# Two pairs of score banks in turn, a mask written by TensorE, an expert split in the attention steps, and another order in the last layer

## The chip, the cores and the metric

One NeuronCore of a Trainium2 chip runs the whole program. The metric is the device time of one execution in microseconds (us). TensorE (PE) multiplies, VectorE (DVE), ScalarE (ACT) and GpSimd (POOL) do the elementwise work, SyncE (SP) only issues DMAs. Each engine runs its own instruction list in order and waits for the others on semaphores. PSUM, into which TensorE writes, has eight banks of 128 x 512 float32.

## The reference

The input is x (1024 tokens of 256 values, four sequences of 256), token ids and a context of four 256 x 256 matrices. Four blocks are added to x in turn, each on a layer-normalised input:

```
x = x + experts_by_token_id(norm(x), ctx)          # stage A: silu(x.W)*(x.W) @ W, 4 experts
x = x + [attention(16 heads of 16, causal) + MoE(8 experts of 512, best 2)](norm(x))   # B, M
x = x + wkv_recurrence(norm(x), ctx)               # stage C: scans over 256 positions
x = x + bitlinear(gelu(bitlinear(norm(x), w1)), w2)  # stage D: 256 -> 1024 -> 256
```

In the attention, scores above the diagonal are minus infinity before the softmax. In stage D each row of the input and of the gelu's output is scaled by 127 over its largest magnitude and rounded.

## The kernel before

Tokens are cut into 8 tiles of 128. Every engine has its program written out by hand. There is no planner, so an instruction runs when all before it in its engine's list have and its semaphores stand.

**Attention (about 90 to 245 us).** The four sequences are batches b, with 8 pairs of heads each. That makes 32 pairs r. For each pair the scores are computed twice. `score_row_pair(r)` (L1477) writes q.k with queries on the partitions, and `row_max` (L1037) on DVE adds the causal mask and takes each row's maximum, four instructions per pair. All row pairs of batch 0 use banks 0 and 1, those of the other batches banks 2 and 3 (`row_banks`, L380), and a row pair waits until the maxima of the one before it are done. When a batch's 16 heads are done, `max_rows(b)` (L1466) transposes the maxima, `nm_copy` (L759) on ACT negates them, and SP's `store_max` (L449) writes them by DMA as one more row of the packed q. `score_col_pair(r)` (L1495) then gives the transposed scores less their maximum, ACT exponentiates them into `E_sb` (L773), POOL sets the part above the diagonal to 0 (L593 and L595, 2 instructions per head), and `weighted_values` (L1510) multiplies by v.

**The steps.** The first `LEAD` = 12 row pairs run ahead. Then come steps m = 0 to 39 (L1584 on PE, the same loop on the other engines): transposed scores of pair m, row pair m + 12, and for each batch that is finished an epilogue. The epilogue turns the output (`ep_turn_o`, first step of the next batch), divides, turns (`ep_turn_h`, second), multiplies by Wo (`ep_out`, third), normalises (POOL's rs at L603, DVE's x_n at L1139), turns again (`ep_turn_x`, fifth) and computes the router's logits (`ep_logits`, sixth). `max_rows` of batches 1 to 3 stands in steps 4, 12 and 20. DVE splits the weights of experts 0 and 1 into a high and a low part in quarters (`split_piece`, L1154, steps 16 to 19 and 24 to 27). POOL splits expert 2 after the last step (L606).

**Router, MoE and recurrence (245 to 472 us).** DVE and PE sort the tokens by expert, POOL gathers 23 blocks of 128 rows by indirect DMA, PE multiplies each by its expert's weights in three products (L1366 to L1368).

**Stage D (472 to 513 us).** Per tile: DVE normalises and scales (`d_scales`, L1304), POOL rounds (`d_round`, L642), PE turns (`d_h_turn`), ACT copies (`d_h_copy`), PE multiplies by w1 (`d_up_products`), ACT applies gelu, DVE scales, POOL rounds, PE turns (`d_g_turn`), ACT copies (`d_g_copy`), PE multiplies by w2 (`d_down_products`), DVE adds (`d_last`). PE's order in a step is turn, up, down of three tiles back, g turn of two tiles back (L1774). DVE does the scales of tile s and of the gelu output s - 2 in one call.

Of the kernel before, what the change touches and what calls it, by code (L numbers as in the profile page):

```python
# [15 lines left out]
def mixed_block_kernel(nc, x, ids, ctx_t, wqkv_t, wo_t, wr_t, wexp, ln1, ln2, decay, decay_row, bonus, w1_t, w2_t, out):  # L16
    F = mybir.dt.float32
    R = mybir.dt.float32r
    BF = mybir.dt.bfloat16
# [6 lines left out]
    P = 128  # L26
# [25 lines left out]
    with ctx:  # L52
# [23 lines left out]
        causal = sb(base, "causal", [P, 2 * P])  # L76
        iota_p = sb(base, "iota_p", [P, P])
# [100 lines left out]
        junk = sb(scope_b, "junk", [P, 2, 3 * P], BF)  # L178
# [38 lines left out]
        Q_FIRST = 1e-15  # L217
        w_exp = sb(scope_c, "w_exp", [P, KC])
# [6 lines left out]
        q_h = sb(scope_c, "q_h", [P, 2, D])  # L225
# [3 lines left out]
        q_top = sb(scope_c, "q_top", [P, NT + 2, 2])  # L229
        q_unit = sb(scope_c, "q_unit", [P, NT + 2, 2])  # L230
        q_inv = sb(scope_c, "q_inv", [P, NT + 2, 2])
        q_deq = sb(scope_c, "q_deq", [P, NT + 2, 2])
# [67 lines left out]
        mask_done = sem("mask_done")  # L300
# [49 lines left out]
        d_inv = sem("d_inv")  # L350
        d_deq = sem("d_deq")
# [19 lines left out]
        NM_AT = {(b + 1) * HP - LEAD: b for b in range(1, B)}  # L371
# [3 lines left out]
        SPLIT_AT = [2 * HP, 3 * HP]  # L375
        EP_OT, EP_HT, EP_WO, EP_RMS, EP_XT, EP_LG = 1, 2, 3, 4, 5, 6
# [3 lines left out]
        def row_banks(b):  # L380

            return bank[0:2] if b == 0 else bank[2:4]
# [16 lines left out]
        G_LAG = 2  # L399
# [9 lines left out]
        def _(sp):  # L409
# [85 lines left out]
        def _(pool):  # L495
# [24 lines left out]
            g.memset(causal[:, :], 0.0)  # L520
            g.memset(picked[:, :, :], 0.0)
# [22 lines left out]

            link(g.affine_select(out=causal[:, P:2 * P], in_=causal[:, P:2 * P], compare_op=ALU.is_ge,
# [41 lines left out]
            for m in range(NP + HP):  # L587
                if m < NP:
                    for n in (2 * m, 2 * m + 1):
                        pool.wait_ge(exp_done, n + 1)  # L590
                        diag = E_sb[:, n % E_RING, :]
# [13 lines left out]
            pool.wait_ge(st_done, B * H)  # L605
            split_expert(RING - 1)  # L606
# [35 lines left out]
            def d_round(step):  # L642
                if step < NT:
                    pool.wait_ge(d_inv, step + 1)
                    g.tensor_scalar(q_h[:, step % 2, :], q_h[:, step % 2, :], q_inv[:, step, 0:1], MAGIC,
                                    ALU.mult, ALU.add).then_inc(d_hr, 1)
                i = step - G_LAG
                if i >= 0:
                    pool.wait_ge(d_inv, step + 1)
                    g.tensor_scalar(q_g[:, i % 3, :], q_g[:, i % 3, :], q_inv[:, step, 1:2], MAGIC,  # L650
                                    ALU.mult, ALU.add).then_inc(d_gr, 1)
# [15 lines left out]
            for i in range(2, 4):  # L667
                rsqrt(4, i).then_inc(rstd_in[4], 1)
            for step in range(NT + G_LAG):
                d_round(step)  # L670
                if step < 2:
                    rsqrt(4, step + 4).then_inc(rstd_in[4], 1)
                if step == 1:
# [1159 lines left out]
```

## Time and profile before

| what | us |
|---|---|
| median of three runs (lowest to highest) | 510.27 (509.72 to 516.72) |
| the profiled execution, its span | 516.34, 514.6 |
| busy: PE, DVE, POOL, ACT | 369.4, 261.3, 222.3, 152.8 |
| the chain that ended last: PE, DVE, POOL, issue | 53%, 18%, 10%, 7% |
| mean granted TensorE clock | 0.793 of full |

The span is from the first instruction to the last. "Busy" adds up what ran on an engine. The chain follows the last instruction back through whatever released each step, so its shares say on which engine the time lies, while a busy engine beside the chain costs nothing. The granted clock is 1.0 where TensorE ran at 2.4 GHz and 0.5 at 1.2 GHz. In square brackets a timeline row gives the idle time before an instruction and what ended it.

### The profile page before, as it was taken

How to read it: one execution, taken by the hardware profiler on the slowest of the kernel's cores; microseconds unless marked ns; L12 is line 12 of the kernel's file. 1: busy time of each engine (PE TensorE's matmuls, PEld its weight loads, DVE VectorE, ACT ScalarE, POOL GpSimd, SP SyncE). 2: the span in 40 equal slices, each digit the busy share in tenths (PEclk: the TensorE clock that was granted, in tenths of full speed). 3: DMA queues.
4: the chain of work that ended last, by engine and by line, in shares of the span. 5: the costliest groups of instructions: out<-in, count | busy, mean ns of one | idle time of the engine just before them, and what ended most of it. 6: DMA issues, size and time to landing. Idle time of an engine off the chain costs nothing.

```text
span 514.6 us, 6681 instructions
## 1 busy us (share of the span) xinstructions
PE 369.4 (72%) x2042; PEld 282.0 (55%) x2045; DVE 261.3 (51%) x780; ACT 152.8 (30%) x332; POOL 222.3 (43%) x338
## 2 busy tenths in 40 slices
PE   0776999648797877764353399999999535757765
PEld 0555787326565655443342288887788314646454
DVE  4578896654354672514720032333232157998652
ACT  2221243113342425410020134333243311233563
POOL 2482443402232444615277208676930188423530
PEclk9997899757757667755556599999999955786799
DMA  8900029967180004000033334326000132000011
GB/s 260 394 11 1 0 94 155 150 138 120 44 120 25 3 2 144 20 1 20 1 84 109 52 121 176 134 79 221 34 26 29 37 90 62 1 1 0 4 37 42
DMA packets 16693, 39.18 MB, mean 76 GB/s; under 512 B 3314, under 2 KB 10804, under 8 KB 14868
## 3 DMA queue, kind: packets, MB, share of 16 engines
q1 hardware_dynamic: 11476, 30.63, 22.3%
q0 software_dynamic: 1872, 5.11, 3.9%
q10 hardware_dynamic: 3312, 3.02, 1.7%
q8 instruction: 18, 0.29, 0.2%
q14 instruction: 15, 0.12, 0.1%
HBM read 29.38 MB, written 9.31 MB: 75 GB/s over the span
## 4 chain that ended last, share of the span: by engine, by line
PE 53%; DVE 18%; POOL 10%; issue 7%; DMA 5%; ACT 4%; another core or an unknown queue 2%; SPq 1%; ACTq 0%; DVEq 0%; POOLq 0%
PE bank L1366 8%; PE bank L1368 7%; PE bank L1367 7%; PE bank L1372 6%; DVE junk L1045 4%; PE bank L1428 3%; POOL yc L629 3%; PE bank L1489 3%; PE bank L1553 3%; PE bank L1462 2%; PE bank L1525 2%; PE bank L1739 2%; PE bank L1537 2%; PE bank L1758 1%
## 5 line engine op out<-in xcount | busy, mean ns | idle before, releaser
L1241 DVE TENSOR_TENSOR act_lo<-bank,act_hi 128x512 fp32r<-128x512 f32 x23 | 15.9, 692 | 84.9 <-ACT act_hi L815 74.4
L1045 DVE CUSTOM_DVE_ANT_0 junk<-bank,causal 128x128 bf16<-128x128 f32 (+1 forms) x128 | 38.0, 354 | 28.0 <-PE bank L1489 28.0
L593 POOL TENSOR_SCALAR_AFFINE_SELECT E_sb<-E_sb 128x128 f32<-128x128 f32 x64 | 21.3, 333 | 71.5 <-ACT E_sb L773 71.4
L1366 PE MATMUL bank<-we_hi,xg_hi 128*128 x92 | 39.7, 432 | 9.8 <-DVE xg_lo L1235 8.2
L584 POOL TENSOR_TENSOR we_lo<-we_lo,we_hi 128x3072 fp32r<-128x3072 f32 x6 | 40.8, 6798 | 0.5
L1367 PE MATMUL bank<-we_lo,xg_hi 128*128 x92 | 37.3, 405 | 0.0
L1368 PE MATMUL bank<-we_hi,xg_lo 128*128 x92 | 37.2, 404 | 0.0
L1366 PE MATMUL bank<-we_hi,act_hi 128*128 x92 | 28.9, 314 | 10.7 <-DVE act_lo L1241 10.7
L773 ACT ACTIVATE E_sb<-bank 128x384 f32<-128x384 f32 x64 | 27.9, 488 | 24.0 <-PE bank L1507 22.6
L583 POOL TENSOR_SCALAR we_hi<-we_lo 128x3072 fp32r<-128x3072 f32 x6 | 17.0, 2828 | 36.3 <-DMA we_lo<-in_wexp 36.2
L629 POOL DMA_INDIRECT yc<-y_dram,pos_i x16 | 15.9, 991 | 35.7 <-DMA y_dram<-y_sb 31.7
L1489 PE MATMUL bank<-k_pack,q_pack 48*128 48x256 f32 (+1 forms) x128 | 20.8, 413 | 14.0 <-DVE negmax L1045 13.9
L613 POOL DMA_INDIRECT xg<-xn_dram,slot_tok x23 | 22.0, 958 | 17.2 <-DVE slot_tok L1219 10.5
L1368 PE MATMUL bank<-we_hi,act_lo 128*128 x92 | 26.5, 288 | 0.0
L1367 PE MATMUL bank<-we_lo,act_hi 128*128 x92 | 26.5, 288 | 0.0
L1489 PEld LDWEIGHTS bank<-k_pack,q_pack 48*128 48x128 f32 x128 | 13.0, 251 | 24.2 <-DVE negmax L1045 18.1
L1366 PEld LDWEIGHTS bank<-we_hi,act_hi 128*128 128x128 f32 x92 | 17.9, 195 | 15.1 <-issue 14.9
L1366 PEld LDWEIGHTS bank<-we_hi,xg_hi 128*128 128x128 f32 x92 | 18.1, 196 | 12.8 <-issue 10.4
L1248 DVE TENSOR_TENSOR act_m<-sil,bank 128x512 f32<-128x512 f32 x23 | 15.8, 688 | 15.3 <-remote 10.0
L811 ACT ACTIVATE sil<-bank 128x512 f32<-128x512 f32 x23 | 13.8, 598 | 32.7 <-PE bank L1368 25.8
L806 ACT ACTIVATE xg_hi<-bank 128x256 fp32r<-128x256 f32 x23 | 8.8, 384 | 46.3 <-PE bank L1372 34.4
L595 POOL TENSOR_SCALAR_AFFINE_SELECT E_sb<-E_sb 128x128 f32<-128x128 f32 x64 | 21.3, 333 | 0.0
(246 smaller groups left out, 1002.7 us busy)
## 6 DMA issues: line engine op xcount, KB each, us to landing
we_lo<-in_wexp SPq DMA_DIRECT2D x8, 1536.0 KB, 7.1
qk_dram<-qk_parts SPq DMA_DIRECT2D x8, 512.0 KB, 4.3
q_pack<-qk_dram SPq DMA_DIRECT2D x24, 128.0 KB, 4.6
k_pack<-qk_dram SPq DMA_DIRECT2D x24, 128.0 KB, 7.8
y_dram<-y_sb ACTq DMA_DIRECT2D x23, 128.0 KB, 1.7
we_hi<-in_w_t SPq DMA_DIRECT2D x2, 1024.0 KB, 11.1
ctx_sb<-in_ctx_t SPq DMA_DIRECT2D x1, 1024.0 KB, 5.4
xn_dram<-x_n SPq DMA_DIRECT2D x8, 128.0 KB, 1.8
```

The source lines that it names most:

```text
L584: g.tensor_tensor(lo, lo.bitcast(F), hi.bitcast(F), ALU.subtract).then_inc(split_done, 1)
L593: g.affine_select(out=diag[:, 0:P], in_=diag[:, 0:P], compare_op=ALU.is_ge, fill=0.0, base=0, pattern=[[1, P]], channel_multiplier=-1)
L595: g.affine_select(out=diag[:, 2 * P:3 * P], in_=diag[:, 2 * P:3 * P], compare_op=ALU.is_ge, fill=0.0, base=0, pattern=[[1, P]], channel_mu ...
L613: g.indirect_dma_start(xg[:, s, :], None, xn_dram, bass.IndirectOffsetOnAxis(slot_tok[:, s:s + 1], 0))\
L629: g.indirect_dma_start(yc[:, i % YB, c, :], None, y_dram, bass.IndirectOffsetOnAxis(pos_i[:, c, i:i + 1], 0))\
L773: a.activation(E_sb[:, n % E_RING, :], bank[4 + n % 2][:, 0:3 * P], ACT.Exp).then_inc(exp_done, 1)
L1045: last = v.tensor_tensor_reduce(out=junk[:, m % 2, t * P:t * P + keys], in0=row_banks(b)[h % 2][:, t * P:t * P + keys], in1=causal[:, 2 * ...
L1366: t_.matmul(dst, l_hi, r_hi, start=start, stop=False)
L1367: t_.matmul(dst, l_hi, r_lo, start=False, stop=False)
L1368: return t_.matmul(dst, l_lo, r_hi, start=False, stop=stop)
L1372: last = t_.transpose(dst[:, k * P:(k + 1) * P], src[:, k * P:(k + 1) * P], ident[:, :] if idt is None else idt)
L1489: last = t_.matmul(row_banks(b)[odd][:, t * P:t * P + (t + 1) * P], q[parts[odd], j, t * P:(t + 1) * P], k[parts[odd], j, 0:(t + 1) * P], ...
```

## The change

1. **Row pairs.** The 12 row pairs ahead use banks 0/1 and 2/3 in turn, and a row pair waits only for the maxima of the pair two before it. From row pair 12 on banks 2/3 are used, each after the one before. `max_rows` writes into bank 7 and stands one step later (5, 13, 21), with waits for what else uses that bank. In the part ahead, `b_low(5)`, `b_norm(6)`, `b_norm(7)` on DVE and `b_turn(6)`, `b_turn(7)` on PE move behind more row pairs.
2. **Mask.** `score_col_pair` first writes the mask into each of the two banks with a bf16 product of the identity and a constant 128 x 384 matrix (0 or -1e30), and the scores are accumulated on it. POOL's 128 instructions on `E_sb` go. POOL makes the constant at the start (one memset, two selects).
3. **Epilogue.** `ep_turn_x` and `ep_logits` stand one step later (sixth and seventh).
4. **Expert 2.** Its load is issued once the transposed scores of batch 1 are done, and DVE splits experts 0, 1, 2 in steps 18 to 21, 22 to 25, 26 to 29. POOL's split of it goes.
5. **Stage D.** The input's scales are separate from those of the gelu output and run three tiles ahead on three buffers. PE's order in a step is g turn, turn of the next tile, down, up of the next tile, and ACT's is gelu, copy of the next tile, g copy.

The added wait on `nm_row` in the diff stands in `ep_logits`; the last two blocks are DVE's and PE's loops of stage D.

```diff
+        causal_t = sb(base, "causal_t", [P, 3 * P], BF)
-        NM_AT = {(b + 1) * HP - LEAD: b for b in range(1, B)}
+        NM_AT = {(b + 1) * HP - LEAD + 1: b for b in range(1, B)}
-        SPLIT_AT = [2 * HP, 3 * HP]
-        EP_OT, EP_HT, EP_WO, EP_RMS, EP_XT, EP_LG = 1, 2, 3, 4, 5, 6
+        SPLIT_AT = [2 * HP + 2, 2 * HP + 6, 3 * HP + 2]
+        EP_OT, EP_HT, EP_WO, EP_RMS, EP_XT, EP_LG = 1, 2, 3, 4, 6, 7
+        def row_banks(r):
+            return bank[0:2] if r < LEAD and r % 2 == 0 else bank[2:4]
+        def row_bank_free(r):
+            return 2 * (r - 1) if r < LEAD else 2 * r
...
             store_max(2)
             for i in range(TB):
                 store_x2(i)
+            sp.wait_ge(st_done, 2 * H)
+            load_expert(RING - 1)
             store_max(3)
...
-            sp.wait_ge(st_done, 3 * H)
-            load_expert(RING - 1)
...
+            g.memset(causal_t[:, :], 0.0)
+            for c in (0, 2):
+                g.affine_select(out=causal_t[:, c * P:(c + 1) * P], in_=causal_t[:, c * P:(c + 1) * P],
+                                compare_op=ALU.is_ge, fill=-BIG, base=0, pattern=[[1, P]], channel_multiplier=-1)
...
-                if m < NP:
-                    for n in (2 * m, 2 * m + 1):
-                        pool.wait_ge(exp_done, n + 1)
...
-                        g.affine_select(out=diag[:, 0:P], in_=diag[:, 0:P], compare_op=ALU.is_ge, fill=0.0,
-                                        base=0, pattern=[[1, P]], channel_multiplier=-1)
-                        g.affine_select(out=diag[:, 2 * P:3 * P], in_=diag[:, 2 * P:3 * P], compare_op=ALU.is_ge,
-                                        fill=0.0, base=0, pattern=[[1, P]], channel_multiplier=-1)\
-                            .then_inc(mask_done, 1)
...
-            pool.wait_ge(st_done, B * H)
-            split_expert(RING - 1)
...
-                if r >= 1:
-                    pe.wait_ge(max_done, 2 * r)
+                if r == 1:
+                    pe.wait_ge(a_y_in, NT)
+                elif r >= 2:
+                    pe.wait_ge(max_done, row_bank_free(r))
...
                 for odd in range(2):
-                    t_.matmul(bank[4 + odd][:, 0:S], k[parts[odd], j, 0:P], q[parts[odd], j, :], start=True, stop=True)
+                    t_.matmul(bank[4 + odd][:, 0:3 * P], ident_b[:, :], causal_t[:, :], start=True, stop=False)
+                for odd in range(2):
+                    t_.matmul(bank[4 + odd][:, 0:S], k[parts[odd], j, 0:P], q[parts[odd], j, :], start=False, stop=False)
...
-                pe.wait_ge(mask_done, 4 * g + 4)
+                pe.wait_ge(exp_done, 4 * g + 4)
...
+                pe.wait_ge(nm_row, min(bt + 3, B))
...
-            for r in range(5, HP):
+            for r in range(2, 9):
                 score_row_pair(r)
             max_rows(0)
-            for r in range(HP, LEAD):
-                score_row_pair(r)
+            score_row_pair(9)
+            b_turn(6)
+            score_row_pair(10)
+            b_turn(7)
+            score_row_pair(11)
...
+            for i in range(NT + 2):
+                if i < NT:
+                    d_g_scales(i)
+                if i + H_AHEAD < NT:
+                    d_h_scales(i + H_AHEAD)
+                if i >= 2:
+                    d_last(i - 2)
...
-                if step < NT:
-                    d_h_turn(step)
-                    d_up_products(step)
-                if step >= G_LAG + 1:
-                    d_down_products(step - G_LAG - 1)
-                if G_LAG <= step < NT + G_LAG:
-                    d_g_turn(step - G_LAG)
+                if 2 <= step < NT + 2:
+                    d_g_turn(step - 2)
+                if step + 1 < NT:
+                    d_h_turn(step + 1)
+                if step >= 3:
+                    d_down_products(step - 3)
+                if step + 1 < NT:
+                    d_up_products(step + 1)
```

## Rows read from the trace of the kernel before

**Rows 1.** Stages: start:end, span, busy PE, PEld, DVE, ACT, POOL; clock; DMA share; GB/s
```profile
90.00:116.50 26.50, 13.77 (x66) 8.58 (x66) 16.18 (x96) 3.51 (x6) 5.90 (x8) 0.63 0.78 144
116.50:222.00 105.50, 86.95 (x600) 59.53 (x598) 52.08 (x246) 40.25 (x93) 40.54 (x130) 0.69 0.27 57
258.00:292.00 34.00, 11.88 (x46) 9.51 (x46) 4.88 (x16) 4.50 (x8) 22.03 (x23) 0.60 0.38 89
292.00:407.00 115.00, 110.93 (x645) 92.98 (x646) 36.36 (x63) 39.58 (x85) 53.54 (x18) 0.99 0.27 95
472.00:514.00 42.00, 27.91 (x171) 19.00 (x174) 21.88 (x56) 21.59 (x41) 13.12 (x16) 0.87 0.07 26
```

**Rows 2.** Timeline 20 to 60 us, POOL and DVE: start, length, instruction, idle before
```profile
27.79 0.28 POOL L545 TENSOR_SCALAR_AFFINE_SELECT causal<-causal 128x128 f32<-128x128 f32 x1
...
35.39 0.43 DVE L923 BATCH_NORM_STATS2 stat<-x_sb 128x6 f32<-128x256 f32 x1 [1.29 <-POOL x_sb L562]
```

**Rows 3.** Page, costliest groups: busy, mean ns, idle before and its releaser
```profile
L1045 DVE CUSTOM_DVE_ANT_0 junk<-bank,causal 128x128 bf16<-128x128 f32 (+1 forms) x128 | 38.0, 354 | 28.0 <-PE bank L1489 28.0
```

**Rows 4.** Timeline 100 to 120 us, TensorE and the sync queue
```profile
107.04 0.79 PE L1489 MATMUL bank<-k_pack,q_pack 48*128 48x128 f32 x4 [1.29 <-DVE negmax L1045]
...
109.13 0.60 PE L1469 MATMUL bank<-ident,negmax 128*16 128x128 f32 x2 [1.29 <-DVE negmax L1045]
...
116.50 0.42 PE L1505 MATMUL bank<-q_pack,k_pack 49*128 49x256 f32 x2
...
110.16 1.46 SPq L453 DMA_DIRECT2D q_pack<-negmax_t  x2
```

**Rows 5.** Waits 117 to 245 us: who waited for whom, us, times, longest
```profile
PE bank L1372 <- DVE x_n L1139: 10.1, 2, 6.7
...
PE bank L1469 <- DVE negmax L1045: 7.3, 3, 2.7
...
PE bank L1525 <- POOL E_sb L595: 2.2, 2, 1.7
```

**Rows 6.** Timeline 180 to 192 us, the step before the maxima are turned
```profile
188.28 0.35 DVE L1131 SCALAR_TENSOR_TENSOR rs_tmp<-mv 128x1 f32<-128x1 f32 x2
...
189.79 0.60 PE L1469 MATMUL bank<-ident,negmax 128*16 128x128 f32 x2 [2.74 <-DVE negmax L1045]
```

**Rows 7.** Timeline 478 to 486 us, TensorE: bf16 products at either clock
```profile
478.70 1.89 PE L1739 MATMUL bank<-w1q,q_ht 128*128 128x512 bf16 x4 [0.47 <-ACT q_ht L883]
...
483.75 1.04 PE L1739 MATMUL bank<-w1q,q_ht 128*128 128x512 bf16 x4 [1.03 <-ACT q_ht L883]
484.62 1.04 PE L1758 MATMUL bank<-w2q,q_gt 128*128 128x256 bf16 x8
```

**Rows 8.** Timeline 212 to 250 us, DVE and POOL: normalised rows, gate, split
```profile
215.31 0.92 DVE L1139 SCALAR_TENSOR_TENSOR x_n<-res,rs,ln_row 128x256 f32<-128x256 f32 x2 [0.58 <-POOL rs L603]
...
237.75 3.37 DVE L1139 SCALAR_TENSOR_TENSOR x_n<-res,rs,ln_row 128x256 f32<-128x256 f32 x2 [1.09 <-POOL rs L603]
...
245.77 1.89 DVE L1179 TENSOR_TENSOR gate<-top 128x8 f32<-128x8 f32 x1
...
248.83 0.17 DVE L1191 TENSOR_TENSOR gate<-gate 128x8 f32<-128x8 f32 x1
...
237.80 3.05 POOL L583 TENSOR_SCALAR we_hi<-we_lo 128x3072 fp32r<-128x3072 f32 x1
```

**Rows 9.** Timeline 485 to 510 us, the last layer: DVE, ACT, TensorE
```profile
485.77 1.22 DVE L1316 TENSOR_REDUCE q_top<-q_g 128x1 f32<-128x1024 f32 x1 [1.96 <-ACT q_g L892]
...
487.76 0.41 DVE L928 TENSOR_SCALAR q_h<-x_sb,mv,rs 128x256 f32<-128x256 f32 x1
...
486.57 1.09 ACT L900 ACTIVATE q_gt<-bank 128x512 bf16<-128x512 f32 x2 [0.83 <-PE bank L1372]
...
487.99 1.04 PE L1739 MATMUL bank<-w1q,q_ht 128*128 128x512 bf16 x3 [1.24 <-ACT q_ht L883]
...
507.75 1.05 PE L1758 MATMUL bank<-w2q,q_gt 128*128 128x256 bf16 x8 [1.18 <-ACT q_gt L900]
```

More of the change, by code:

```diff
@@ L217, in mixed_block_kernel @@
         Q_FIRST = 1e-15
+        H_AHEAD = 3
+        H_BUF = 3
         w_exp = sb(scope_c, "w_exp", [P, KC])
@@ L666, in _ @@
             c_times_v(3)
-            for i in range(2, 4):
+            for i in range(2, 5):
                 rsqrt(4, i).then_inc(rstd_in[4], 1)
[L669 to L673, printed above, removed]
-                    for i in range(6, 8):
-                        rsqrt(4, i).then_inc(rstd_in[4], 1)
+            for i in range(H_AHEAD):
+                d_round_h(i)
+                rsqrt(4, i + 5).then_inc(rstd_in[4], 1)
+            for i in range(NT):
+                d_round_g(i)
+                if i + H_AHEAD < NT:
+                    d_round_h(i + H_AHEAD)
         @block.scalar
@@ L762, in nm_copy @@
                     act.wait_ge(nm_in[b - 1], 32)
-                a.activation(negmax_t[:, :], row_banks(b)[0][0:H, 0:S], ACT.Copy, scale=-1.0).then_inc(nm_row, 1)
+                a.activation(negmax_t[:, :], bank[EP_Z][0:H, 0:S], ACT.Copy, scale=-1.0).then_inc(nm_row, 1)
             nm_copy(0)
+            b_turned(6)
+            b_turned(7)
             for m in range(NP + HP):
@@ L902, in d_g_copy @@
                 last.then_inc(d_gtc, 1)
-            for step in range(NT + G_LAG):
+            d_h_copy(0)
+            for step in range(NT + 2):
                 if step < NT:
-                    d_h_copy(step)
                     d_gelu_of(step)
-                if step >= G_LAG:
-                    d_g_copy(step - G_LAG)
+                if step + 1 < NT:
+                    d_h_copy(step + 1)
+                if step >= 2:
+                    d_g_copy(step - 2)
         @block.vector
@@ L1097, in _ @@
             b_low(4)
-            b_norm(6)
-            b_stats(7)
-            row_pair(1)
-            row_pair(2)
-            b_low(5)
-            row_pair(3)
+            row_pair(1)
+            b_stats(7)
+            for r in range(2, 6):
+                row_pair(r)
+            b_low(5)
+            for r in range(6, 8):
+                row_pair(r)
+            b_norm(6)
+            row_pair(8)
             b_norm(7)
-            for r in range(4, LEAD):
+            for r in range(9, LEAD):
                 row_pair(r)
@@ L1349, in _ @@
                 c_result(i)
[L1350 to L1357 removed]
+                if i < 4 + H_AHEAD:
+                    d_h_scales(i - 4)
+            for i in range(NT + 2):
+                if i < NT:
+                    d_g_scales(i)
+                if i + H_AHEAD < NT:
+                    d_h_scales(i + H_AHEAD)
+                if i >= 2:
+                    d_last(i - 2)
         @block.tensor
@@ L1467, in max_rows @@
                 pe.wait_ge(max_done, H * (b + 1))
+                if b == 0:
+                    pe.wait_ge(b_lo, 6)
+                elif b == 1:
+                    pe.wait_ge(b_lo, 2 * B)
+                else:
+                    pe.wait_ge(ep_htc, b - 1)
                 for t in range(TB):
-                    last = t_.transpose(row_banks(b)[0][0:H, t * P:(t + 1) * P], negmax[:, b % 2, t, :], ident[:, :])
+                    last = t_.transpose(bank[EP_Z][0:H, t * P:(t + 1) * P], negmax[:, b % 2, t, :], ident[:, :])
                 last.then_inc(nm_tr, 1)
```

109 lines of the change are left out of this document (44 added, 65 removed).

## The prediction

> **What bounds the kernel now.** I read the stages first, then the waits, then the timelines of the stretches that the change touches. By stage [rows 1], TensorE is busy for 110.93 of 115 us in the experts at nearly full clock. Nothing in the change touches that, and the 34 us at their start belong to gathers and waits that it leaves alone. Three stretches are loose. In the row pairs ahead of the steps (90 to 116.5 us) PE is busy for 13.8 of 26.5 us. In the steps (116.5 to 222) it is busy for 87 of 105.5 us at a mean clock of 0.69, so PE mostly sets the pace, and its work there is dear. In the last layer it is busy for 28 of 42 us. The reader should see why each is loose. Ahead of the steps PE and DVE take turns: a row pair starts every 2.09 us (107.04 to 109.13), 1.29 of them spent waiting for maxima [rows 4]. In the steps PE's waits are few and have names [rows 5]. After the last step DVE works beside a long POOL split and is slow [rows 8].
>
> **Base.** The sum is made against the profiled execution, 516.34 us with a span of 514.6. It is 6.1 us above the median of 510.27, which two of the three runs are near. I take the difference between the kernels off the median.
>
> **1. Two bank pairs: -6.2 us.** DVE needs 38.0 us for 32 pairs of maxima, 1.19 us a pair [rows 3]. With two bank pairs PE's 0.8 us [rows 4] fit beside that. The first two pairs don't gain, since PE runs a projection product between pair 1 and pair 2 as before, and counting back five periods from 107.04 puts pair 2 at 97 and its maxima at 97.6. From there DVE has six pairs and one 0.7 us copy until batch 0's maxima are done: 97.6 + 7.1 + 0.7 = 105.5, against 109.1 before. Then come the transposes 0.6, the copy 0.4, the issue 1.46 (before at 110.16), and a landing, which no row shows for so small a transfer. The nearest is 1.7 us for 128 KB. That gives 109.7. The DMA engines are 78% busy here [rows 1] with the packed heads, so I take 110.3 for the first transposed scores, which before started at 116.50. Bounds: 4 (the row waits behind all the head loads) to 7.5 (it does not wait). The norms and turns of tiles 6 and 7 lie under DVE's and PE's slack. Their users (steps 1 and 3) come more than 6 us later, and if they were late the product at step 1 would be what waits.
>
> **2. Maxima turned a step later: -4.0 us.** PE waited 7.3 us for the maxima at steps 4, 12 and 20 [rows 5]. What is late next is the v product of the same step. At step 4, which has 7.3 - 2 x 2.7 = 1.9 of it, nothing else holds it, so 1.8 is gained. At 12 and 20 it waits for the residual's statistics, ready at 188.28 + 0.35, while the transposes started at 189.79 [rows 6]. So 1.1 is gained at each. The maxima row now has three steps, some 5 us, to reach the packed q before its batch starts. Transposes, copies, issue and landing as in part 1 are 4.2 us, or 5.1 behind an exponential. That is bounded by 0 and 1.5 us lost at each of three batches; I take 0. Expert 2's load now stands in SP's queue ahead of the last `store_max`, but it waits for scores five steps older, so that queue isn't held. The router's new wait on the maxima copy is met two steps before it.
>
> **3. Epilogue a step later, no POOL in the softmax: -2.9 us.** For batch 2, PE waited 3.4 us (10.1 less 6.7) for x_n [rows 5], which is made at 215.31 to 216.2 [rows 8] and will be no earlier. But the transposed scores of step 30 (two pairs of products as at 116.50 [rows 4], 0.75 us) now come before that wait. The 1.7 us wait for POOL's masking at the end and the 0.5 us one at step 24 go [rows 5]. Elsewhere masking was hidden and removing it is worth nothing; what covered it was PE's own row of work. For batch 3 nothing overlaps before or after.
>
> **4. Expert 2 split by DVE: -4.2 us.** The last x_n pair takes 3.37 us beside POOL's split, which begins 0.05 us after it, and 0.92 otherwise: 2.45. The gate's first operation takes 1.89 and its sister 0.17: 1.7 [rows 8]. Both are on the chain to the router. The four split pieces cost DVE some 6 us in steps 26 to 29, where before the pieces of expert 1 stood in steps 24 to 27. DVE is busy for 52 of 105 us there [rows 1], so they cost 0 to 1; I take 0.
>
> **5. Last layer: -8.0 us.** One step is 4.24 us (483.75 to 487.99), of which PE idles 1.24 [rows 7, 9], because ACT's copy for the next product stands behind two g copies (1.09), and those stand behind PE's g turn. In the new order PE needs 3 x 0.87 + 0.2 = 2.8 us, ACT 21.6 / 8 = 2.7 [rows 1]. DVE needs 2.0 for the g scales and the last add (485.77 to 487.76), and 1.2 for the scales of the input (a 0.41 us normalisation, a reduction as long, three small ones), together 3.2, which is the bound while input tiles last. Four steps at 3.2 save 4.2 (I carry 4.4, since DVE's lag has one step of slack), and the first step without ACT's g copies in front 0.8. At the end a step is 3.1 us (two PE groups of 0.87, the 1.18 wait and latencies [rows 9]). Now the down product runs beside the next g copy, 2.2 us a step, three times: 2.8. Sum 8.0. Bounds: 4 (POOL's rounding, twice as many waits, becomes the chain) to 10.
>
> **6. Constant: +0.5 us.** Two selects of 0.25 to 0.28 us stand on POOL ahead of the work for which DVE waited 1.29 us [rows 2]. The memset falls into idle time.
>
> **7. The mask on PE: +11.5 us.** Each step gets two products of 384 bf16 columns. Four products of 512 take 0.87 us at full clock (483.75 to 484.62), and the row at half clock shows 1.89 against 1.04 [rows 7]. So 384 columns are 0.16 or 0.32 us, and a step gets 0.32 or 0.64. They stand behind the wait for the exponential and before the scores, so they lengthen that loop too. At 0.69 mean clock some 38% of the steps' time is at full clock, so the mean is about 0.52. Seven of the 32 steps have a longer wait on PE anyway (step 2 for maxima, 12 and 20 for statistics, 26 for h_tok, 28 to 30 for x_n), and steps 6, 8 and 16 are paced by the row maxima. That leaves 25 x 0.52 = 13 less 1.5. Bounds: 6.5 (all at full clock) and 20.5 (all at half clock, nothing hidden).
>
> **Sum.** -6.2 - 4.0 - 2.9 - 4.2 - 8.0 + 0.5 + 11.5 = -13.3. From 516.3 that is 503.0 in the profiled execution, and from the median 510.3 it is **497 us**. (About 2%, 10 us, is what a measurement of this kernel tells from no change.)
>
> **The clock in the sum.** The same four products run at 1.2 GHz at 478.70 and at 2.4 GHz at 483.75, 5 us of PE work later [rows 7]. In the steps the mean is 0.69, between the two levels [rows 1]. The Trainium skill, TensorE: Matmul & The Clock Gate, Part 1, says the half rate is the default state and that activity releases it. By that rule the added products would partly pay for themselves. By the rows alone no such gain is taken, and it is the second rival below.
>
> **Rivals.**
> - *The mask is hardly hidden, or a new wait eats a gain:* 20.5 instead of 11.5, or the maxima rows late by 1.5 us three times. 510.3 - 24.8 + 20.5 = 506, with the middle of the case at 505. For it: PE busy 87 of 105.5 us. Against: the named waits. 22%.
> - *The clock rises:* the steps' PE work at half clock is 87 x 0.6 = 52 us. If 40% of it ran at full clock 10 us would go, and the mask would cost 9: 510.3 - 24.8 + 9 - 10 = 485, middle 487. For it: fewer gaps, more columns. Against: PE is busy 82% of the steps already and the mean is still 0.69 [rows 1]. 18%.
> - *The clock falls (the slower end):* PE stays at 1.2 GHz through all the steps. The 38% at full clock, 33 us, double; the 18.5 us of idle time absorb half of that, the mask costs 20.5: 510.3 - 24.8 + 20.5 + 15 = 521. It decides once more than about two thirds of the full-clock stretches are lost. For it: only the loss of the runs of products in which the clock rose, as waits move. 5%.
> - *It does not do what it says:* the last layer is still paced by gelu, scale, round, turn in series, and the row pairs by the head loads. Only parts 2 to 4 stay, against the mask: 510.3 - 11 + 11 = 510. 5%.
>
> The forecast has 50%, with 491 to 503 as its own range. **Range:** the ends are the clock's rise and the dear mask, 485 to 509, which leaves out about 2 in 10. **Chances:** faster by over 2% needs under 500.1: 0.43 of the forecast's 0.50, the clock's rise, a little of the dear mask: 0.64. Within 2%: 0.31. Slower: 0.05.
>
> **What would show it.** The first transposed scores near 110 us instead of 116.5. No POOL line on E_sb. No PE wait for negmax after step 0. x_n after the last step at 0.92 and the gate near 0.2 us. Stage D steps of about 3.2 and then 2.2 us. Steps from the first transposed scores to the last 5 us longer or no shorter than 105. What would make it wrong: a granted clock in the steps off 0.69 by more than 0.1, PE waits for the DMA of the maxima row, or a longer stretch between the first gather and the second block of the experts (34 us now), in which no engine works much.

## The result and the profile after

The kernel after takes **484.72 us** (477.54 to 485.66, 4 runs) against 512.02 us (509.72 to 516.72, 4 runs) of the kernel before: a ratio of 0.938, 95% interval 0.921 to 0.955. The forecast was 497 us with a range of 485 to 509, so the gain was 27 us where 13 were forecast, and the time lies 0.3 us under the range. A ratio with an interval, here and below, compares the mean times of each kernel's fast runs (those at most 1.5% above its quickest), while a median is of all its runs, so a ratio need not be the quotient of the medians beside it. The profiled execution of the kernel after took 484.51 us, span 482.8. That of the kernel before took 516.34, 4.3 us above its median, so the stretches below add up to 31.8 us, 4.5 more than the medians differ.

The page of the kernel after: busy shares, then TensorE's busy tenths and its granted clock in 40 slices of the span.

```profile
PE 366.7 (76%) x2106; PEld 275.4 (57%) x2109; DVE 262.1 (54%) x806; ACT 152.8 (32%) x332; POOL 175.5 (36%) x211
...
PE   0786899868988989753542899998999616786696
...
PEclk9997899857799799655575699999999855777699
```

I cut both executions at the same five events: first row pair, first product into the banks of the transposed scores, last weighted values, first gather, first up product of the last layer, end. Columns: stretch, its length, busy time of PE, PEld, DVE, ACT, POOL, granted clock, DMA share, GB/s. First the kernel before:

```profile
90.50:116.50 26.00, 13.27 (x64) 8.41 (x65) 16.18 (x96) 3.51 (x6) 5.40 (x8) 0.62 0.77 139
116.50:225.00 108.50, 88.37 (x616) 60.12 (x614) 52.08 (x246) 41.07 (x94) 41.57 (x134) 0.69 0.27 56
225.00:258.10 33.10, 14.21 (x61) 11.28 (x57) 17.02 (x50) 1.79 (x4) 10.65 (x5) 0.50 0.02 8
258.10:472.90 214.80, 159.04 (x861) 131.52 (x863) 91.35 (x195) 58.95 (x127) 111.91 (x97) 0.83 0.24 75
472.90:514.60 41.70, 27.90 (x171) 18.85 (x172) 21.05 (x54) 21.17 (x39) 13.12 (x16) 0.87 0.07 26
```

And the kernel after:

```profile
89.40:108.70 19.30, 12.26 (x63) 7.95 (x62) 15.35 (x95) 2.54 (x6) 5.38 (x8) 0.66 0.80 163
108.70:204.20 95.50, 86.10 (x680) 52.56 (x678) 57.61 (x256) 42.23 (x95) 3.61 (x6) 0.88 0.35 69
204.20:233.10 28.90, 14.20 (x61) 11.27 (x57) 12.83 (x49) 1.79 (x4) 0.88 (x2) 0.50 0.03 10
233.10:449.10 216.00, 161.88 (x860) 133.59 (x862) 91.80 (x200) 59.08 (x127) 112.40 (x98) 0.81 0.24 75
449.10:482.80 33.70, 26.59 (x171) 18.47 (x172) 22.50 (x67) 20.84 (x39) 12.42 (x15) 0.90 0.10 32
```

| stretch | before | after | measured | forecast |
|---|---|---|---|---|
| up to the first row pair | 90.5 | 89.4 | -1.1 | 0.5 |
| row pairs (part 1) | 26.0 | 19.3 | -6.7 | -6.2 |
| steps (parts 2, 3, 7) | 108.5 | 95.5 | **-13.0** | **+4.6** |
| to the first gather (part 4) | 33.1 | 28.9 | -4.2 | -4.2 |
| experts and recurrence | 214.8 | 216.0 | +1.2 | 0 |
| last layer (part 5) | 41.7 | 33.7 | -8.0 | -8.0 |
| span | 514.6 | 482.8 | -31.8 | -13.3 |

The second row of each fence is the one to read: 64 products more (680 against 616) and yet less PE time (86.10 against 88.37), because the clock is 0.88 instead of 0.69. Four other rows came near their forecasts, two of them by another way than forecast (see below). The first row of the table is within the scatter of the kernels below (89.3 to 92 us).

PE's waits in the kernel after, 89 to 245 us (who for whom, us, times, longest), answer to [rows 5]: no wait for the maxima to be turned and none for POOL. Row pairs still wait for the maxima before them (L1499).

```profile
PE bank L1499 <- DVE negmax L1044: 5.1, 8, 1.3
PE bank L1376 <- DVE x_n L1141: 5.0, 2, 4.2
...
PE bank L1515 <- ACT E_sb L770: 3.2, 7, 1.0
...
PE bank L1499 <- DMA k_pack<-qk_dram: 2.3, 1, 2.3
PE bank L1466 <- DVE rs_tmp L1133: 2.2, 2, 1.1
```

PE's timeline of the row pairs and of one step of the last layer, and DVE's behind the last step, answer to [rows 4, 7, 8] (start, length, instruction, idle before it and its releaser):

```profile
98.71 0.70 PE L1499 MATMUL bank<-k_pack,q_pack 48*128 48x128 f32 x4 [0.62 <-DVE negmax L1044]
99.82 0.79 PE L1499 MATMUL bank<-k_pack,q_pack 48*128 48x128 f32 x4 [0.41 <-DVE negmax L1044]
...
104.05 0.80 PE L1499 MATMUL bank<-k_pack,q_pack 48*128 48x128 f32 x4 [2.32 <-DMA k_pack<-qk_dram]
104.78 0.59 PE L1479 MATMUL bank<-ident,negmax 128*16 128x128 f32 x2
...
108.72 0.82 PE L1515 MATMUL bank<-causal_t,ident_b 128*128 128x384 bf16 x2
...
461.30 1.03 PE L1750 MATMUL bank<-w1q,q_ht 128*128 128x512 bf16 x3
...
464.13 1.03 PE L1750 MATMUL bank<-w1q,q_ht 128*128 128x512 bf16 x4
...
473.75 1.09 PE L1376 MATMUL bank<-ident,q_g 128*128 128x128 f32 x8 [0.39 <-POOL q_g L647]
...
476.73 1.09 PE L1376 MATMUL bank<-ident,q_g 128*128 128x128 f32 x8 [1.02 <-POOL q_g L647]
```

```profile
216.94 0.88 DVE L1141 SCALAR_TENSOR_TENSOR x_n<-res,rs,ln_row 128x256 f32<-128x256 f32 x2 [1.09 <-POOL rs L603]
...
222.48 0.17 DVE L1181 TENSOR_TENSOR gate<-top 128x8 f32<-128x8 f32 x1
```

Row pairs follow each other in 1.11 us, x_n takes 0.88 and the gate 0.17 us, and a step of the last layer 2.83 us.

### The profile page after: what moved, and what is told of

Read it like the earlier page. It is cut to its first block, busy times and chain, and to the rows that moved or that the text cites. A ratio compares the mean times of both kernels' runs of the same rounds, so it can differ in the third digit from the quotient of the medians.

```text
span 482.8 us, 6716 instructions
## 1 busy us (share of the span) xinstructions
PE 366.7 (76%) x2106; PEld 275.4 (57%) x2109; DVE 262.1 (54%) x806; ACT 152.8 (32%) x332; POOL 175.5 (36%) x211
## 4 chain that ended last, share of the span: by engine, by line
PE 51%; DVE 17%; POOL 10%; DMA 6%; issue 5%; another core or an unknown queue 4%; ACT 3%; SPq 2%; POOLq 0%; ACTq 0%; DVEq 0%
PE bank L1370 9%; PE bank L1371 8%; PE bank L1372 8%; PE bank L1376 6%; POOL yc L627 3%; PE bank L1432 3%; PE bank L1515 2%; PE bank L1537 2%; PE bank L1565 2%; PE bank L1499 2%; PE bank L1466 2%; DMA k_pack<-qk_dram 2%; PE bank L1517 1%; DMA we_lo<-in_wexp 1%
## 5 line engine op out<-in xcount | busy, mean ns | idle before, releaser
L1044 DVE CUSTOM_DVE_ANT_0 junk<-bank,causal 128x128 bf16<-128x128 f32 (+1 forms) x128 | 37.5, 353 | 17.5 <-PE bank L1499 17.5
L602 POOL TENSOR_SCALAR rs_tmp<-rs_tmp 128x2 f32<-128x2 f32 x4 | 1.0, 254 | 113.2 <-DVE rs_tmp L1133 113.2
L594 POOL TENSOR_TENSOR we_lo<-we_lo,we_hi 128x3072 fp32r<-128x3072 f32 x5 | 34.1, 6818 | 0.4
L593 POOL TENSOR_SCALAR we_hi<-we_lo 128x3072 fp32r<-128x3072 f32 x5 | 13.9, 2778 | 37.2 <-DMA we_lo<-in_wexp 37.2
L808 ACT ACTIVATE sil<-bank 128x512 f32<-128x512 f32 x23 | 13.8, 598 | 32.6 <-PE bank L1372 25.6
L1499 PE MATMUL bank<-k_pack,q_pack 48*128 48x256 f32 (+1 forms) x128 | 18.0, 369 | 7.5 <-DVE negmax L1044 5.1
L1432 PE MATMUL bank<-h_t,wqkv 128*128 128x256 f32 x64 | 18.8, 446 | 2.3 <-DVE qk_parts L1019 2.3
L1372 PEld LDWEIGHTS bank<-we_hi,xg_lo 128*128 128x128 f32 x92 | 18.1, 197 | 4.2
## 6 DMA issues: line engine op xcount, KB each, us to landing
qk_dram<-qk_parts SPq DMA_DIRECT2D x8, 512.0 KB, 4.7
```

Source lines behind the costliest of these rows:

```text
L594: g.tensor_tensor(lo, lo.bitcast(F), hi.bitcast(F), ALU.subtract).then_inc(split_done, 1)
L1044: last = v.tensor_tensor_reduce(out=junk[:, m % 4, t * P:t * P + keys], in0=row_banks(m // 2)[h % 2][:, t * P:t * P + keys], in1=causal[:, ...
L1372: return t_.matmul(dst, l_lo, r_hi, start=False, stop=stop)
L1432: last = t_.matmul(bank[7][:, m * S:(m + 1) * S], wqkv[:, k, qk * D + m * P:qk * D + (m + 1) * P], h_t[:, k, b * S:(b + 1) * S], start=(k ...
L1499: last = t_.matmul(row_banks(r)[odd][:, t * P:t * P + (t + 1) * P], q[parts[odd], j, t * P:(t + 1) * P], k[parts[odd], j, 0:(t + 1) * P], ...
```

## The experiments

Fourteen runs in four sessions, each with the kernel before beside it. In each, "steps" is the stretch from the first product into the transposed scores' banks to the last weighted values, in the one execution that was profiled. The kernel after has steps of 95.5 us, of 94.1 (after_again) and, with nothing changed in them, of 97.7 (u_last). A difference of less than some 3.5 us between two such stretches is therefore not shown.

| kernel | us, median | before beside it | ratio, 95% | steps us, clock |
|---|---|---|---|---|
| after (result above) | 484.7 | 512.0 | 0.938 (0.921 to 0.955) | 95.5, 0.88 (before: 108.5, 0.69) |
| b_pemask | 505.1 | 512.8 | 0.977 (0.967 to 0.986) | 100.3, 0.87 |
| u_poolmask | 493.1 | 512.8 | 0.958 (0.949 to 0.966) | 107.4, 0.66 |
| u_nomask | 483.3 | 512.8 | 0.940 (0.933 to 0.946) | 98.4, 0.73 |
| m_double | 482.8 | 512.8 | 0.939 (0.932 to 0.946) | 94.5, 0.98 |
| b_filler | 505.0 | 512.9 | 0.983 (0.976 to 0.990) | 101.0, 0.87 |
| u_poolfill | 491.5 | 512.9 | 0.956 (0.948 to 0.963) | 106.0, 0.81 |
| v_mask256 | 487.4 | 512.9 | 0.950 (0.940 to 0.959) | 98.5, 0.84 |
| x_tailfill | 478.7 | 512.9 | 0.933 (0.926 to 0.941) | 94.2, 0.98 |
| u_last | 474.4 | 490.1 | 0.963 (0.953 to 0.974) | 97.7, 0.85 |
| u_split | 469.7 | 490.1 | 0.960 (0.949 to 0.971) | 95.4, 0.88 |
| x_allfill | 468.6 | 490.1 | 0.954 (0.946 to 0.963) | 94.0, 0.98 |
| after_again | 462.2 | 493.9 | 0.936 of the medians | 94.1, 0.89 |
| x_endfill | 459.9 | 493.9 | 0.942 (0.934 to 0.950) | 94.2, 0.98 |
| u_poolfill_s | 470.7 | 493.9 | 0.965 (0.953 to 0.977) | 96.7, 0.89 |

Times of different sessions are not compared, only ratios and stretches. In the last two sessions (from u_last down) a stall of some 20 us at the start of the experts was absent from every profiled execution (see the end). In the last session the medians of x_endfill and u_poolfill_s are 0.931 and 0.953 of the median beside them, to be set against the 0.936 of after_again. For b_pemask and b_filler the interval excludes 1, but not a gain of less than 2%.

**The mask alone, undone or done.**

```diff
 # u_poolmask: after, with
+                for n in (2 * m, 2 * m + 1):      # POOL: the two affine_selects on E_sb, then mask_done
-                    t_.matmul(bank[4 + odd][:, 0:3 * P], ident_b[:, :], causal_t[:, :], start=True, stop=False)
 # b_pemask: before, with the reverse of this, and the constant made by POOL at the start
```

> The kernel after, with the mask back on POOL as in the kernel before (two selects on E_sb for each head, no mask product on PE); all other parts stay. In the steps the kernel after has 17.5 us of mask products among 86 us of PE work at a mean clock of 0.87, where before it was 88 us at 0.69. Theory A (the mask's columns lift the clock): without them the steps fall back to about 0.69 and the other 69 us of PE work cost what they did before, 88 us; the steps last 100 to 104 us instead of 95.6, the run 490 us or more. Theory B (the waits that went lift it: the moved maxima, the epilogue a step later, the row pairs): the clock stays above 0.83 and the mask's own price comes off, 64 x 0.21 = 13 us less what is hidden, 10 us: 474 us.

> The kernel before with one part of the change alone: the causal mask of the transposed scores by two bf16 products a step on PE, no selects on POOL in the steps. Theory A (columns lift the clock): the steps' clock rises from 0.69 to 0.80 or more, the products pay for themselves, and the run is within 1% of before, 505 to 513 us. Theory B (the waits that went lift it): the clock stays at 0.69, the products cost 25 x 0.52 = 13 us less the 2.2 us of waits for POOL: 521 us.

Both times came as theory A has it: 493.1 us with the clock back at 0.66, and 505.1 us with the clock at 0.87. The steps of u_poolmask are longer than its 100 to 104 us, which u_nomask below explains in part. One line for each kernel's steps:

```profile
109.80:217.20 107.40, 90.14 (x616) 60.84 (x614) 58.55 (x256) 41.97 (x95) 46.15 (x134) 0.66 0.31 61
```

```profile
116.60:216.90 100.30, 84.75 (x680) 52.70 (x678) 51.60 (x246) 41.59 (x94) 3.61 (x6) 0.87 0.29 60
```

The part that was forecast to cost the most gains 8.2 us of the steps on the kernel before, by itself, and 11.9 in the order of the other parts.

**More and less of it.**

```diff
 # u_nomask: after, the mask product taken out, nothing in its place (no mask: a part of the computation is left out)
-                    t_.matmul(bank[4 + odd][:, 0:3 * P], ident_b[:, :], causal_t[:, :], start=True, stop=False)
 # m_double: after, with this ahead of the mask product
+                for odd in range(2):
+                    t_.matmul(bank[4 + odd][:, 0:3 * P], ident_b[:, :], causal_t[:, :], start=True, stop=True)
 # v_mask256: after, blocks 0 and 2 of the mask alone, scores in three products of 128 columns
+                    t_.matmul(bank[4 + odd][:, :].rearrange("p (c w n) -> p c w n", c=2, w=2)[:, :, 0, :],
+                              ident_b[:, :], causal_t[:, :].rearrange("p (c n) -> p c n", c=2), start=True, stop=False)
```

> The kernel after with no mask on the transposed scores at all, neither on PE nor on POOL (this leaves out part of the computation: future keys take part in the attention). It prices the mask as a whole. Theory A: the clock in the steps falls to about 0.69 and the run is 488 us or more, slower than the kernel after although it does less. Theory B: 474 us at a clock above 0.83. If it agrees with the kernel with POOL's mask within 2 us, POOL's selects were hidden.

> The kernel after with the mask products issued twice (the first pair is overwritten by the second, same result). Theory A: the clock in the steps rises further, from 0.87 towards 0.95, and the 64 added products cost 5 us or less: 485 to 490 us. Theory B: they cost their duration at the clock as it is, 64 x 0.21 = 13 us less a few hidden: 495 us.

> The kernel after with a cheaper mask: the middle third of the mask is zeros, so each mask product has 256 columns instead of 384, and the scores are three products of 128 columns instead of two. 128 columns fewer at 0.053 us each are 64 x 0.053 = 3.4 us of PE. If the products only cost their time: 481 us. If their columns hold the clock up, a third fewer lose some of it: the steps' clock falls from 0.87 to 0.75 to 0.82, and the run is 484 to 488 us.

The steps of u_nomask, m_double and v_mask256:

```profile
109.40:207.80 98.40, 84.43 (x616) 57.56 (x614) 57.72 (x258) 41.84 (x95) 3.60 (x6) 0.73 0.34 67
```

```profile
110.90:205.40 94.50, 87.70 (x744) 54.34 (x742) 57.56 (x256) 41.95 (x95) 3.60 (x6) 0.98 0.34 70
```

```profile
109.40:207.90 98.50, 89.61 (x744) 58.45 (x742) 57.59 (x256) 42.34 (x95) 3.61 (x6) 0.84 0.33 67
```

With no, one and two pairs of products a step the clock is 0.73, 0.88 and 0.98, and the steps take 98.4, 95.5 and 94.5 us. The clock follows the products. The time does not get longer by them, and that it gets shorter is not shown here: the steps differ by hardly more than their scatter, and the whole runs stand at 0.940, 0.938 and 0.939 of the kernel before. So in this order the products pay for themselves, and theory A's misses are two: m_double took 482.8 us, not 485 to 490, and u_nomask took 483.3 us, not 488 or more. Its steps are 9 us shorter than with POOL's selects, which I had called hidden. v_mask256 did not get the 3.4 us that its shorter products save; its steps are 3 us longer, which is within the scatter, at a clock of 0.84 where 0.75 to 0.82 was expected. As it also has 64 products more of another shape, it does not tell how much of that is the clock.

**Products for nothing.** b_pemask changed two things, products added and selects gone. b_filler keeps the selects and adds only work.

```diff
 # b_filler: before, with this ahead of the transposed scores, which overwrite it (u_poolfill: the same on u_poolmask)
+                for odd in range(2):
+                    t_.matmul(bank[4 + odd][:, 0:3 * P], ident_b[:, :], causal_t[:, :], start=True, stop=True)
```

> The kernel before, POOL's masking kept, with the two bf16 products of 384 columns added in each step where the mask products stand in the kernel after, but overwritten by the scores: work for nothing. It tells the two things apart that b_pemask changed together, the added columns and POOL's selects gone. Theory A1 (the columns lift the clock): steps at 0.80 or more, the other 88 us of PE work shrink to about 69 as in b_pemask, and the run is 504 to 510 us, faster than before with more work. Theory A2 (the selects' absence does it): the clock stays at 0.69 to 0.73 and the products cost 13 us: 520 to 526 us.

> The kernel u_poolmask (after, with the mask back on POOL), with the same two overwritten bf16 products a step. A1: the clock rises from 0.66 to 0.85 or more, steps 97 to 100 us against 107.4, run 483 to 487 us. A2: the clock stays below 0.75 and the run is 500 us or more. What stays above the kernel after is the price of waiting for POOL's selects, 2 to 4 us.

b_filler settles the cause: 64 products whose results nobody reads, and that take nothing off any engine, make the kernel before 1.7% faster. Its steps, then three groups of products in its steps (busy us, mean ns, idle before), and the same three in the kernel before:

```profile
116.20:217.20 101.00, 84.71 (x680) 52.67 (x678) 51.95 (x246) 41.52 (x94) 42.49 (x134) 0.87 0.29 60
```

```profile
L1510 PE MATMUL bank<-causal_t,ident_b 128*128 128x384 bf16 x64 | 17.2, 354 | 3.8 <-ACT E_sb L778 3.8
...
L1532 PE MATMUL bank<-E_sb,v_aug 128*32 128x256 f32 x128 | 11.6, 440 | 1.7 <-POOL E_sb L600 1.7
L1467 PE MATMUL bank<-wqkv,h_t 128*128 128x256 f32 x32 | 11.4, 521 | 0.0
...
L1560 PE MATMUL bank<-wo,ho_t 128*128 128x256 f32 x24 | 6.0, 392 | 0.0
```

```profile
L1525 PE MATMUL bank<-E_sb,v_aug 128*32 128x256 f32 x128 | 14.1, 525 | 2.2 <-POOL E_sb L595 2.2
L1462 PE MATMUL bank<-wqkv,h_t 128*128 128x256 f32 x32 | 13.3, 591 | 0.0
...
L1553 PE MATMUL bank<-wo,ho_t 128*128 128x256 f32 x24 | 9.4, 560 | 0.0
```

The added products are busy for 17.2 us, and the others shrink from 88.4 to 84.7 - 17.2 = 67.5. Of the 7.5 us by which the steps get shorter, 3.7 are busy time of PE, and the rest is less waiting. Taking POOL's selects away as well (b_pemask) brings 0.7 us more, which is within the scatter.

u_poolfill missed: clock 0.81, but steps of 106.0 us, where 97 to 100 were expected. POOL's timeline in it, next to DVE's:

```profile
206.10 1.04 POOL L604 TENSOR_SCALAR_AFFINE_SELECT E_sb<-E_sb 128x128 f32<-128x128 f32 x1
...
209.15 0.29 POOL L606 TENSOR_SCALAR_AFFINE_SELECT E_sb<-E_sb 128x128 f32<-128x128 f32 x1
```

```profile
206.03 0.96 DVE L1172 TENSOR_TENSOR we_lo<-we_lo,we_hi 128x768 fp32r<-128x768 f32 x1
```

```profile
209.00 1.08 PE L1548 MATMUL bank<-E_sb,v_aug 128*32 128x256 f32 x8 [2.85 <-POOL E_sb L606]
```

A select takes 0.29 us alone and 1.04 beside DVE's pieces of an expert, and part 4 had put four more pieces into the steps. So I formed theory C and tried it.

```diff
 # u_poolfill_s: u_poolfill with part 4 undone (u_split: the same on the kernel after)
-        SPLIT_AT = [2 * HP + 2, 2 * HP + 6, 3 * HP + 2]
+        SPLIT_AT = [2 * HP + 2, 3 * HP]
+            pool.wait_ge(st_done, B * H)
+            split_expert(RING - 1)
```

> u_poolfill (after, mask on POOL, overwritten products on PE) with expert 2 split by POOL behind the last step, as in the kernel before. In u_poolfill the steps took 106.0 us although its products are those that gave 101.0 in b_filler; POOL's selects took 0.29 us, but up to 1.04 us each in steps where DVE splits experts, PE waited 4.1 us for them and the clock fell to 0.58 to 0.61 in those stretches. Theory C (DVE's four added pieces stretch the selects, and the waits drop the clock): without them the steps take 98 to 101 us and the clock is 0.85 or more; the stretch behind the last step is 4.2 us longer. If the selects are late for another reason, the steps stay at 105 us or more.

```profile
109.50:206.20 96.70, 85.21 (x680) 52.12 (x678) 52.35 (x248) 42.22 (x95) 42.30 (x134) 0.89 0.35 68
```

It holds: 96.7 us at 0.89, where 98 to 101 were expected, and 32.9 us behind the last step. By the profiled executions DVE's added pieces cost the steps 9.3 us while POOL masks: PE waits 4.1 us for POOL with them and 1.8 without, and is busy for 92.6 and 85.2 us. But the execution of u_poolfill that was profiled was the slowest of its four, and that of u_poolfill_s the fastest. By the medians the gain over the kernel before is 21.3 and 23.3 us, which with the 4.0 us lost behind the last step makes some 6 us. Once PE masks they cost nothing that can be seen, as the next kernel shows.

**Parts 4 and 5 undone in the kernel after.**

> The kernel after with expert 2 split by POOL behind the last step, as before, and DVE's pieces for expert 1 where they were. Forecast term: 4.2 us, from x_n and the gate alone: the stretch from the last weighted values to the first gather goes from 28.9 to 33 us, run 489 us. If the four added DVE pieces had cost the steps something, the steps get shorter than 95.5 us by up to 2 and the run is 487 us.

> The kernel after with the last layer's order of before (input scales, rounding, copies and products in common steps with the gelu side, its buffers and semaphores as before); all else stays. Forecast term: 8.0 us. If the order is what shortened it, the stretch from the first up product to the end goes from 33.7 back to 41.5 us and the run to 492 us. The rival, that the stretch shrank because its clock rose from 0.87 to 0.90, gives at most 27.9 x 0.03 = 1 us: then the run is 486 us.

u_last takes the old loops of the last layer back, on all engines. ACT's is one of them:

```diff
-                if step + 1 < NT:
-                    d_h_copy(step + 1)
+                if step < NT:
+                    d_h_copy(step)
```

By stretches both are as forecast: with u_split the steps stay at 95.4 us and the stretch to the first gather is 33.1 instead of 28.9; with u_last the last layer is 41.3 us at a clock of 0.90, so the order and not the clock shortened it. The expected times of whole runs, 489 and 492 us, do not apply, since the third session lacked the stall.

**Filling the gaps elsewhere.**

```diff
 # x_tailfill: m_double, with fill(n) ahead of waits behind the last step, n = 3, 6, 3, 23, 3, 9, 26, 26
+            def fill(n):
+                for _ in range(n):
+                    t_.matmul(bank[4][:, 0:3 * P], ident_b[:, :], causal_t[:, :], start=True, stop=True)
```

> The kernel with the doubled mask products, and behind the last step the same kind of overwritten product in each gap where PE waits, sized to the gap at full clock: 3, 6, 3, 23 and 3 before the five pieces of the last batch's epilogue, 9 before the ranks, 26 before the slots, 26 before the first expert block (0.16 us each). In that stretch the kernel after runs at 0.50 and PE works 14 us on its chain. If the clock holds at full through it, that becomes 7 to 8: the stretch from the last weighted values to the first gather goes from 25.6 us (kernel with doubled products) to 21 or 22, run 479 us. If the clock falls anyway, the added products take 0.32 instead of 0.16 us and stand in the way: 488 us or more.

> The kernel with doubled mask products and filled gaps behind the last step (x_tailfill), and overwritten products of the same kind in five more places where PE waits and the work behind ran at half clock: 8 in the last row pairs, 40 before the third block of the experts, 8, 4, 18 and 12 in the recurrence's outputs, 13, 6 and 3 before the first up products. If each stretch then runs at full clock, it saves 1 us in the first steps (clock 0.78), 2.5 in the first blocks (6 us of PE work at half clock), 2 in the first recurrence outputs, 3 at the start of the last layer: 470 us. If PE is not on the path in these places or the clock falls anyway, it stays within 2 us of x_tailfill, 477 to 481 us.

> The kernel after itself, beside the kernel before, in the same session as the two below. The runs of the third batch stood beside a kernel before of 490 us instead of 512, because a stall of 20 us at the start of the experts was absent from their records (first gather to first up product of the last layer 194 to 195 us instead of 212 to 216). If the change's gain is independent of that stall, the difference to before is 24 to 29 us in either case, a ratio of 0.938 to 0.951.

> x_tailfill (doubled mask products, gaps behind the last step filled) with 20 instead of 26 ahead of the experts, and 12 overwritten products before the last recurrence outputs, 13, 6 and 3 before the first up products, none in the experts, where the 40 of x_allfill stood in the way once the stall was absent (205 us against 194). From the records: steps 94.2, last weighted values to first gather 24.2, last layer 32.1, against 95.5, 28.9 and 33.7 in the kernel after: 7.6 us faster than the kernel after of the same session, ratio 0.984 to it. If the filling does nothing for the chain, it is within 2 us of it.

The stretch behind the last step in x_tailfill:

```profile
204.60:228.70 24.10, 20.59 (x130) 13.54 (x129) 12.81 (x51) 1.79 (x4) 0.91 (x3) 0.96 0.04 12
```

24.1 us against 28.9, at 0.96 against 0.50: 4.8 us, where I expected 7. Only 1.5 of it are due to the filled gaps, for in m_double, which has none filled, the stretch is 25.6 us at 0.67. In x_allfill the last layer took 32.1 us at 0.99, against 34.3 in x_tailfill (other kernels with nothing filled there: 32.4 to 33.9), but the experts and the recurrence took 205.3 us against 194.3 in u_split of the same session, so the products added there cost more than they gave, and its expected 470 us, made with the stall in it, was met only because the stall was absent. That most of it is due to the 40 ahead of a block that no longer waits is my guess, not shown. x_endfill leaves these 40 out, and all in the recurrence but 12, and has the stretches that I expected except one (197.1 us in the experts and the recurrence, against 194.1 in after_again). Its runs lie between 458.9 and 461.8 us, those of the kernel after between 453.4 and 467.3 with mean clocks of 0.887 to 0.842. Median against median it is 0.5% faster, which is not shown to be a difference, and the 7.6 us that I expected did not come. They were counted from the result's execution, while in after_again the same three stretches took 94.1, 26.8 and 32.6 us instead of 95.5, 28.9 and 33.7. From there the filling takes 2.9 us off and costs 3.0 in the experts and the recurrence. The gain of the kernel after in the fourth session is 31.8 us by the medians, more than the 24 to 29 expected. It is no smaller without the stall.

## Why the prediction was wrong

**Part 7 failed, by its sign.** "By the rows alone no such gain is taken" is the sentence. It priced the mask at +11.5 us of steps by adding the products' own time at a clock taken as given at 0.69. The same products, added to the kernel before with nothing else changed in the steps (b_filler), made the steps 7.5 us shorter. With the 2.2 us of waits for POOL in part 3 the forecast for b_pemask was +9.3, and it came at -8.2: 17.5 us of the 17.6 by which the steps were missed. The products' own time agrees with the forecast, 17.5 / 32 = 0.55 us a step measured and 0.52 forecast, but by luck. At the measured clock of 0.88 the forecast's own 0.16 and 0.32 us a product give 0.40. A pair took 0.82 us at half clock (at 108.72 above), and at full clock:

```profile
134.48 0.50 PE L1515 MATMUL bank<-causal_t,ident_b 128*128 128x384 bf16 x2
```

The clock is an outcome of the same instructions: with them it is 0.88, and the other products cost 86.1 - 17.5 = 68.6 us instead of 88.4. This was my second rival, 485 us at 18%, and the sign named for it, a clock off 0.69 by more than 0.1, came. I counted against it that PE was busy 82% of the steps already. That was no argument. Where PE's busy share was highest before, it was at half clock:

```profile
143.00:157.00 14.00, 13.18 (x80) 9.01 (x79) 5.83 (x36) 5.49 (x13) 5.12 (x20) 0.50 0.83 114
```

After, two stretches of 24 us ran at full clock with a share no higher:

```profile
133.00:157.00 24.00, 21.25 (x205) 12.87 (x204) 14.86 (x87) 11.58 (x27) 0.89 (x2) 1.00 0.50 76
157.00:169.00 12.00, 11.19 (x82) 7.04 (x86) 5.61 (x38) 4.33 (x11) 0.00 (x0) 0.72 0.39 140
169.00:193.00 24.00, 21.59 (x198) 13.47 (x190) 20.29 (x54) 11.75 (x28) 0.88 (x2) 1.00 0.04 13
```

A busy PE in this view includes products slowed by the very clock in question, so the share is no argument that the clock cannot rise. The Trainium skill, TensorE: Matmul & The Clock Gate, Part 1, says that the throttled clock is the default and activity releases it. b_filler agrees (0.69 to 0.87 by products for nothing). I had cited that rule and given the rows' silence more weight; a mean between the two levels should have read as a clock that work could still lift.

**Parts 2 and 3** held where the clock did: from b_pemask to the kernel after, both at 0.87 to 0.88, the steps go from 100.3 to 95.5, -4.8 us. The forecast for the two without POOL's 2.2 us was -4.7. That the two agree so closely is luck, as one stretch scatters by more than 3 us. At the old clock the same parts, with part 4, gave 1.1 us (108.5 to 107.4). "No PE wait for negmax after step 0" did not come: row pairs in the steps waited 2.7 us in four places for the maxima before them, as before the change (3.1 us), which the working left out.

**Part 3's "masking was hidden"** failed in the new order. The selects' named waits were 2.2 us, but u_nomask has steps 9.0 us shorter than u_poolmask, and u_poolfill_s shows the pieces of part 4 as a reason for most of it. The parts are not additive: what the moved split costs depends on where the mask is made. The Trainium skill, GPSIMD Engine Reference, Key points, says that POOL shares its interfaces to SBUF (the memory that holds the tiles) with DVE, with contention when DVE has two SBUF inputs; the select of 1.04 us beside DVE's two-input subtraction agrees.

**Part 1** came at -6.7 for -6.2, with a wait that I had not named: 2.32 us for the packed keys of batch 1, in the middle of the row pairs. The path was another than forecast, too: no wait stands before the first transposed scores at 108.72, since PE's own list of row pairs and turns lasted until then, so the maxima row did not set that time, and the near agreement is partly luck.

**Part 4** came at -4.2, as forecast, x_n and the gate at 0.88 and 0.17 us; u_split confirms it. With its steps at 95.4 us it also shows no cost of the pieces there, up to the scatter.

**Part 5** came at -8.0, with other terms: 2.83 us a step instead of 3.2 while there are input tiles, and 2.4 to 3.0 instead of 2.2 at the end, where POOL's rounding is what is late.

**The constant** of part 6 can't be told from the scatter.

## What to carry to other kernels

Where TensorE's mean clock lies between its two levels, price an added product twice: at its own time, and with all other products of the stretch at full clock; cheap work that moves from another engine to TensorE may then have a price of nothing or less, as the mask had here. Test it with products whose results are overwritten, before writing the change. And when a change moves elementwise work between POOL and DVE, look at what each instruction of the one takes beside the other, since parts that seem independent meet there.

## What was not expected of the hardware

- 64 overwritten products of 384 bf16 columns made an otherwise unchanged program 1.7% (1.0 to 2.4%) faster, its steps' clock 0.69 to 0.87.
- The same kernel on one chip ran in 453.4 to 467.3 us, its mean clock going from 0.887 to 0.842 with it. The filled x_endfill, at 0.907 to 0.918, spread 2.9 us in six runs.
- In the executions profiled with the result and in the first two sessions PE, DVE and ACT stood still in turn at the start of the experts, as ACT in the kernel after:

```profile
242.22 0.60 ACT L808 ACTIVATE sil<-bank 128x512 f32<-128x512 f32 x1 [0.88 <-issue]
248.88 0.60 ACT L808 ACTIVATE sil<-bank 128x512 f32<-128x512 f32 x1 [6.06 <-remote]
255.26 0.60 ACT L812 ACTIVATE act_hi<-bank 128x512 fp32r<-128x512 f32 x1 [5.79 <-remote]
```

In after_again, the same program in another session, they did not:

```profile
242.25 0.60 ACT L808 ACTIVATE sil<-bank 128x512 f32<-128x512 f32 x1 [0.73 <-PE bank L1372]
245.00 0.60 ACT L808 ACTIVATE sil<-bank 128x512 f32<-128x512 f32 x1 [2.15 <-PE bank L1372]
245.49 0.59 ACT L812 ACTIVATE act_hi<-bank 128x512 fp32r<-128x512 f32 x1
```

That is 22 us (216.0 against 194.1 from the first gather to the first up product). POOL did not stand still: its 23 gathers, one every 1.25 us, run from 233.1 to 261.9 us in both. The first and the third session ran on the same chip, with the stall and without it. "remote" and "issue" name nothing in the program that the engines waited for, and no run here was made to find it: its cause stays open.
